# The message sum of the recurrence as two fp32r products per graph instead of one fp32 product

## The reference: four graph layers in a row

```python
A = (adj != 0).astype(x.dtype)
h = x
for l in range(weight.shape[0]):            # 5 passes
    m = jnp.einsum('bnd,de->bne', h, weight[l])
    agg = jnp.einsum('bij,bid->bjd', A, m)  # sum over the in-neighbours
    h = _gru_cell(agg, h, w_ih, w_hh, b_ih, b_hh)
```

## Time and profile before

| | |
|---|---|
| median of 3 executions | 786.51 us (783.95 to 788.78) |
| the profiled execution, own time | 786.21 us |
| its span, first to last instruction | 784.4 us |
| PE busy | 691.5 us (88%), x4091 |
| PEld busy | 583.5 us (74%) |
| DVE busy | 599.7 us (76%), x1461 |
| ACT busy | 521.8 us (67%) |
| POOL busy | 298.6 us (38%) |
| mean granted PE clock | 0.965 of full |

### The profile page before, as it was taken

The page is one execution under the profiler, slowest core; times in us unless marked ns, Lnnn a source line. Parts: engine busy times, 40 slices in busy tenths (PEclk is TensorE's granted clock), DMA queues, the critical chain, the costliest instruction groups (busy, mean ns, idle before and its releaser), DMA issues.

```text
span 784.4 us, 12359 instructions
## 1 busy us (share of the span) xinstructions
PE 691.5 (88%) x4091; PEld 583.5 (74%) x4091; DVE 599.7 (76%) x1461; ACT 521.8 (67%) x1083; POOL 298.6 (38%) x423
## 2 busy tenths in 40 slices
PE   3899899989999979989999989989999989975765
PEld 2678588878888768878888767878788867865544
DVE  4688997888978966888978977888976877876143
ACT  5566677578778766668768757767767656646533
POOL 4222424573334343363343343463332242453320
PEclk9999989999999999999999999999999999999769
DMA  6600011100000020300000020210000000200001
GB/s 152 167 26 1 2 35 25 51 2 4 8 1 1 1 57 21 116 28 3 7 3 1 1 57 10 72 28 4 6 3 1 1 1 1 80 28 7 5 1 55
DMA packets 47623, 21.08 MB, mean 27 GB/s; under 512 B 9032, under 2 KB 47560, under 8 KB 47560
## 3 DMA queue, kind: packets, MB, share of 16 engines
q1 hardware_dynamic: 47560, 20.29, 9.6%
HBM read 15.27 MB, written 4.19 MB: 25 GB/s over the span
## 4 chain that ended last, share of the span: by engine, by line
PE 43%; DVE 30%; ACT 13%; POOL 8%; issue 5%; DMA 1%; DVEq 0%; SPq 0%; POOLq 0%; ACTq 0%
PE bank L404 7%; PE bank L405 7%; PE bank L406 6%; PE bank L399 5%; DVE zd L1292 4%; DVE hd L1304 4%; DVE h L1296 4%; DVE bank L1318 3%; DVE rh L1315 3%; POOL rstd L908 2%; PE bank L593 2%; ACT bank L880 2%; ACT xn L689 2%; PE bank L528 2%; DVE h_hi L1299 2%
## 5 line engine op out<-in xcount | busy, mean ns | idle before, releaser
L924 POOL TENSOR_TENSOR h_lo<-h,h_hi 128x512 fp32r<-128x512 f32 x64 | 81.8, 1279 | 339.8 <-DVE h_hi L1299 339.8
L404 PE MATMUL bank<-h_hi,whh_hi 128*128 128x512 f32 x240 | 106.7, 445 | 13.3 <-DVE rh L1315 12.8
L1315 DVE SCALAR_TENSOR_TENSOR rh<-bank,rh 128x512 f32<-128x512 f32 x80 | 55.0, 687 | 68.6 <-ACT bank L874 68.6
L404 PE MATMUL bank<-g_hi,wc_hi 128*128 128x512 f32 x240 | 103.6, 432 | 0.7 <-DVE h L1296 0.3
L406 PE MATMUL bank<-h_lo,whh_hi 128*128 128x512 f32 x240 | 96.3, 401 | 0.0
L405 PE MATMUL bank<-h_hi,whh_lo 128*128 128x512 f32 x240 | 96.1, 401 | 0.0
L405 PE MATMUL bank<-g_hi,wc_lo 128*128 128x512 f32 x240 | 94.9, 395 | 0.0
L406 PE MATMUL bank<-g_lo,wc_hi 128*128 128x512 f32 x240 | 94.8, 395 | 0.0
L399 PEld LDWEIGHTS bank<-edge,hn 128*128 128x128 f32 x640 | 83.6, 191 | 8.2 <-issue 1.0
L689 ACT ACTIVATE xn<-x_res,shift,rstd 128x128 f32<-128x128 f32 x128 | 55.8, 485 | 48.7 <-POOL shift L910 48.7
L399 PE MATMUL bank<-edge,hn 128*128 128x128 f32 x640 | 84.3, 274 | 0.8 <-ACT hn L859 0.8
(11 more groups left out here) (167 smaller groups left out, 1605.9 us busy)
## 6 DMA issues: line engine op xcount, KB each, us to landing
x_in<-in_x SPq DMA_DIRECT2D x8, 512.0 KB, 5.4
adj_in<-in_adj SPq DMA_DIRECT2D x8, 512.0 KB, 4.8
x_res<-in_x SPq DMA_DIRECT2D x16, 256.0 KB, 2.8
out_x<-x_res SPq DMA_DIRECT2D x16, 256.0 KB, 2.3
xz<-x_res SPq DMA_DIRECT2D x16, 50.0 KB
w_sb<-in_L_gnn_W SPq DMA_DIRECT2D x1, 640.0 KB, 5.1
w_sb<-in_L_gnn_W SPq DMA_DIRECT2D x5, 128.0 KB, 5.0
rows<-in_adj SPq DMA_DIRECT2D x32, 0.6 KB
```

The costliest lines, as they stand in the source:

```text
L404: nc.tensor.matmul(dst[:], w_hi, m_hi, start=start, stop=False)
L924: nc.gpsimd.tensor_tensor(h_lo[q][:], h[q][:], h_hi[q][:].bitcast(f32), ALU.subtract).then_inc(sem["h_lo_new"], 1)
L1315: nc.vector.scalar_tensor_tensor(rh[:], R_BANK[:], 1.0, rh[:], ALU.add, ALU.mult).then_inc(sem["rh_ready"], 1)
```

## The change

`hn` (fp32) is replaced by `hn_hi` and `hn_lo` (fp32r), and `edge` becomes fp32r. ACT writes the upper part instead of the full copy. DVE gets one new instruction per step, which subtracts the upper part from the transposed state in `TG` and writes the rest. PE makes two fp32r products of 128 columns per graph, eight instructions a step, and waits for DVE's instruction where it waited for ACT's.

```diff
-        edge = sb("edge", [128, RG, 128])
+        edge = sb("edge", [128, RG, 128], f32r)
...
-        hn = sb("hn", [128, QUAD, 128])
+        hn_hi, hn_lo = sb("hn_hi", [128, QUAD, 128], f32r), sb("hn_lo", [128, QUAD, 128], f32r)
...
-                pe.wait_ge(sem["hn_ready"], n + 1)
-                for j in range(QUAD):
-                    last = nc.tensor.matmul(TG[:, j * 128:(j + 1) * 128], hn[:, j, :], edge[:, q * QUAD + j, :],
-                                            start=True, stop=True)
+                pe.wait_ge(sem["hn_lo_ready"], n + 1)
+                for j in range(QUAD):
+                    nc.tensor.matmul(TG[:, j * 128:(j + 1) * 128], hn_hi[:, j, :], edge[:, q * QUAD + j, :],
+                                     start=True, stop=False)
+                    last = nc.tensor.matmul(TG[:, j * 128:(j + 1) * 128], hn_lo[:, j, :], edge[:, q * QUAD + j, :],
+                                            start=False, stop=True)
...
-                nc.scalar.activation(hn[:], quad(TG[:, :]), ACT.Copy).then_inc(sem["hn_ready"], 1)
+                nc.scalar.activation(hn_hi[:], quad(TG[:, :]), ACT.Copy).then_inc(sem["hn_hi_ready"], 1)
...
+            def turned_lo(n):
+                dve.wait_ge(sem["hn_hi_ready"], n + 1)
+                nc.vector.tensor_tensor(hn_lo[:], quad(TG[:, :]), hn_hi[:].bitcast(f32), ALU.subtract).then_inc(sem["hn_lo_ready"], 1)
+
+            turned_lo(0)
             aggregate_lo(0)
             for n in range(ALL):
+                if n + 1 < ALL:
+                    turned_lo(n + 1)
                 beside(2 * n)
```

More of the change, by code:

```diff
@@ L156, in graph_stack @@
             "blocks_turned", "normT_ready",
-            "hx_ready", "hx_hi", "hx_lo", "h_new", "h_hi_new", "h_lo_new", "h_turned", "hn_ready", "g_made", "g_hi_ready",
+            "hx_ready", "hx_hi", "hx_lo", "h_new", "h_hi_new", "h_lo_new", "h_turned", "hn_hi_ready", "hn_lo_ready", "g_made", "g_hi_ready",
             "g_lo_ready", "gates_r", "gates_h", "hb_ready", "gates_n", "gates_z", "r_ready", "z_ready",
```

## The result

| | before | after |
|---|---|---|
| median of 4 executions | 785.37 us (783.95 to 788.78) | 808.87 us (807.80 to 809.82) |
| ratio, with its 95% interval | | 1.0249 (1.021 to 1.0289) |
| span of the profiled execution | 784.4 us | 808.0 us |
| mean granted PE clock in it | 0.965 | 0.942 |

A forecast was written before the change was run, and what follows sets the result against it. The prediction had PE and DVE taking turns as bound (43% and 30% of the chain of waits). To 786.2 us it added 12.1 + 5.6 + 1.4 = 19.1, no saving, giving 805.3; forecast 806 us, own range 796 to 822, wider 782 to 840.

The forecast's parts named there:

- PE's saving of 0: Aggregate on PE: eight fp32r records a step stay 0.111 us apart, the weight load time, so PE saves 0.
- DVE's 57 us and 655 us busy: DVE: 80 subtractions at 0.72 us a step, 57 us in all; busy time rises from 600 to 655 us.
- The aggregate waits for DVE's queue, 12.1 us: Aggregate starts late behind DVE's queued work and the subtraction, in steps 7 to 10, 12 and two per later round: 12.1 us.
- `rh` moves back, 5.6 us: `rh` later where DVE had no idle: 3.3 us at step 24 over three rounds, 2.3 in steps 1, 18, 38, 58, 78.
- Bare steps, 1.4 us: Steps 2 to 6 and 13 to 16: DVE's loop of 5.68 us against 5.53, 0.15 us each, 1.4 us in sum.
- the tail is only shifted: After step 79: no subtraction is left, so the tail only starts later.
- 1: Rival, aggregate on PE: narrow fp32r products are 0.234 us apart, about 865 us; chance 0.15 together with 5.
- 2: Rival, aggregate on PE: fp32r loads at streaming distance, eight records 0.46 us, 34 us off PE, 771 us; chance 0.08.
- 4 (DVE the bound everywhere): Rival, DVE: all 57 us of the subtractions show, 843 us; chance 0.07.
- 3 (hidden): Rival, DVE: its 68.6 us of idle before `rh` hides the subtraction, less than 8 us left, about 790 us; chance 0.10.
- 5: Rival, PE: fp32r products issued as two records each, 1280 records, 71 us more; folded into 1, together 0.15.

The follow-up runs named there:

- load64: Kernel before with two fp32r products per graph, low part zero, no subtraction, and only 64 of 128 stationary columns in the aggregate's products: 774.03 us, ratio 0.9837.
- move64: Kernel before with two fp32r products per graph, low part zero, no subtraction, and only 64 of 128 moving columns in the aggregate's products: 784.18 us, ratio 0.9953.
- dve_wait: Kernel before, fp32 products kept, with DVE's subtraction added and the aggregate waiting for it, its result unused: 805.2 us, ratio 1.0198.
- dve_nowait2: Kernel before, fp32 products kept, with a 676 ns DVE reduction in the subtraction's place, the aggregate not waiting for it: 801.47 us, ratio 1.0149.
- tiny_wait: Kernel before, fp32 products kept, with a subtraction of 4 columns in place of 512, the aggregate waiting for it: 797.99 us, ratio 1.011.
- shift: Kernel before with three DVE reductions of 0.67 us added at the end of setup: 791.67 us against 790.21, ratio 1.0019.
- pe_only: Kernel before with two fp32r products per graph, low part a tile of zeros made once, no subtraction in the steps: 789.09 us, ratio 0.9984.
- after_beside: Changed kernel with the subtraction moved behind DVE's beside work, directly ahead of `rh`: 825.34 us, ratio 1.0449.

## Why the prediction came out near, step by step

**PE's saving of 0: right.** The distance is 0.111 us with fp32r as with fp32, set by the load (`load64` 0.06, `move64` 0.11), and PE's part alone is worth 0.9984, not to be told from 1. The early second record saves 0.05 us in steps that hang on PE: in steps 27 to 29, 47 to 49 and 67 to 69 the changed kernel gains 0.04 or 0.05 us each, `dve_wait` nothing. That is under 1 us in all.

**DVE's 57 us and 655 us busy: a little high.** The instruction's 0.69 us was right (682 ns). But from its start to the next DVE instruction's start it is 0.60 us, and not the 0.72 that was taken. This is DVE's timeline in steps 3, 8 and 24 of the changed kernel:

```profile
56.02 0.68 DVE L1314 TENSOR_TENSOR hn_lo<-bank,hn_hi 128x512 fp32r<-128x512 f32 x1
56.62 0.68 DVE L1324 SCALAR_TENSOR_TENSOR rh<-bank,rh 128x512 f32<-128x512 f32 x1
...
62.25 0.68 DVE L1324 SCALAR_TENSOR_TENSOR rh<-bank,rh 128x512 f32<-128x512 f32 x1
...
85.63 0.87 DVE L1009 BATCH_NORM_STATS2 stats<-x_in 128x6 f32<-128x128 f32 x4
86.41 0.68 DVE L1314 TENSOR_TENSOR hn_lo<-bank,hn_hi 128x512 fp32r<-128x512 f32 x1
...
213.28 0.69 DVE L1314 TENSOR_TENSOR hn_lo<-bank,hn_hi 128x512 fp32r<-128x512 f32 x1 [0.28 <-ACT hn_hi L861]
213.89 0.28 DVE L1191 BATCH_NORM_STATS2 stats<-xz 100x6 f32<-100x128 f32 x1
```

0.72 is the distance to an instruction that needs the result (`rh` to L1327); the subtraction's successor does not need it and starts 0.09 us before its end. 80 x 0.60 = 48 us, and DVE's busy time rose by 41.8.

**The aggregate waits for DVE's queue, 12.1 us: the step that failed, in size and in place.** Measured in those steps: 2.8 us in steps 7 to 13 (predicted 7.1), and about 2.0 in the six later ones (0.6 in steps 32 and 52, 0.5 in 72, 0.3 in 40; predicted 5.0), 4.8 together. The wait itself exists, and is nearly as large as said: in step 8 PE is idle for 0.86 us for the low part (predicted 1.1). But the prediction compared the aggregate's new start with its old one, and did not ask when PE would have been stopped next. PE's timeline of the kernel before, in the same step, behind the aggregate and the three products of the H part:

```profile
82.53 0.50 PE L404 MATMUL bank<-h_hi,whh_hi 128*128 128x512 f32 x1 [0.37 <-DVE rh L1315]
```

PE waited there anyway, for `rh`, which comes later in DVE's queue than the subtraction. In the changed kernel this product follows without a gap, at 88.83: the lateness of the aggregate has filled the gap. In steps 7 to 12 DVE was the bound before the change, so the cost is DVE's time, 0.6 us a step where it had no idle. `dve_nowait2` and `tiny_wait` show it from both sides (the table by step), and `dve_nowait2` has the same 0.5 to 0.6 us in steps 32, 52 and 72 without any wait. The wait costs where PE had no later stop: 1.0 us in step 13, 0.15 in each bare step, 0.3 each in steps 18, 20 and 40.

**`rh` moves back, 5.6 us: right in the steps that it named, other in its parts, and 2.7 us short elsewhere.** Step 24 and its neighbours (22 to 26, 42 to 46, 62 to 66) gave 1.3, 1.3 and 1.4 us, 4.0 where 3.3 were predicted; from the first the 1.6 us of the fall of the clock at 223 us are taken off. DVE's wait for the copy there was 0.28 us, not 1.2, since DVE's own work ahead of it had become later than the copy had; PE then waited 0.76 us for `rh`, where it had had 0.8 us of slack. Steps 1, 18, 38, 58 and 78 gave 1.6 us (predicted 2.3). Not on the list were 17, 37 and 57 (0.5 each), and 30 and 50 (0.55 each); together with smaller ones, 2.7 us. (What is left of the 14.75 us beside these, the steps above and the bare ones is some 0.5 us, the net of the falls of the clock.)

**Bare steps, 1.4 us: right.** 62.25 - 56.62 = 5.63 us, predicted 5.6 to 5.8; steps 2 to 6 and 14 to 16 gave 1.2 us.

**What was missing: the clock.** The prediction took the clock to be at its upper level in all but the tail; slices of 20 us that say 9 hide the short falls, to 0.50 from 98 to 104, from 299 to 302 and from 654 to 657 us in the kernel before. The sum was 19.1 us; the recurrence gave 14.75. The rest of the 23.6 is 3.8 before step 0 and 5.0 in the tail. Of the 3.8, 0.73 are the aggregate's first wait (`dve_wait` shows them alone); the other 3.1 come with PE's clock at 1.2 GHz from about 29 to 35 us. The prediction's sentence that the tail is only shifted holds for its instructions, not for its time. Eight kernels have a tail of 97.4 to 98.0 us, among them `shift`, which has no part of the change, and five have 92.3 to 92.9, among them the kernel before and `tiny_wait`. These 8 us need none of the change's instructions, as `shift` shows; whether longer steps make the lower clock likelier is not shown. The kernel before itself had a median of 789 to 790 us at a granted clock of mostly 0.950 to 0.959 in the later series, 4 us above the one shown here, so a part of these 8 us, up to about half by the medians, may belong to the quick execution that was recorded of it and not to the change. So the forecast of 806 lies 3 us from the result partly by luck: the recurrence's sum was 4 us too large, and stood in for 8 us of clock that were not in it.

**The rivals.** 1 and 2 fall with `pe_only`. 4 (DVE the bound everywhere) falls with the 46.6 us of idle that are left before `rh`. 3 (hidden) falls too: 48 - 15 = 33 us of the subtraction are hidden, about the two thirds that the forecast implied (57 - 19 = 38), and what is left is twice the 8 us that it allowed. 5 falls with the 320 records of L401.

**Left open.** Why the clock falls after the start in some kernels. The idle of 1.50 us ahead of the first aggregate is not enough for it, as `dve_wait` and `after_beside` have the same idle and stay at 1.00 from 28 to 38 us. In `shift` it falls at 28.2 us, towards the end of an idle of 3.00 us ahead of the first transposes, which lasts 2.55 us in the kernel before and is followed by no fall there. Nor is it shown what decides the length of the tail.

## What to carry to other kernels

An added wait costs only what reaches past the next wait that the waiting engine would have had anyway, so follow the engine to its next stop before pricing the wait. The place of an instruction in an in-order queue can be worth more than the instruction: the same subtraction costs 15, 31 or 65 us of the recurrence in three places. And a gain on one of two engines that take turns is worth about a third of its size here (33 to 36 us off PE gave 12 to 13), while a load on the other came out at about a third as well (48 us on DVE gave 15). And a difference of a few us between two recordings should be checked for falls of the clock, step against like step, before it is given to a cause.

## What the runs showed of the hardware that I had not expected

- A DVE instruction with two inputs in SBUF is stretched from 0.69 to up to 1.72 us when it begins beside a POOL instruction of 512 columns (31 of 80, each ending 0.55 us after POOL's); with one of its inputs in PSUM it is not (at most 0.693 us), nor with a single SBUF input (at most 0.689).
- The granted clock differs between recordings of kernels in work that no edit touches: 0.83 or 0.75 in the tail, worth 5 us; 1.00 or about 0.5 from 29 to 35 us, worth 3; and short falls to 0.50 within the recurrence, worth up to 1.6 us each and 3.9 in all in the kernel before. The kernel before alone took 784.3 to 792.6 us in its 39 later executions. That is as much as many edits are worth.
- An independent successor on DVE starts about 0.09 us before the end of the instruction ahead, a dependent one 0.03 to 0.04 us after it.
